# A three-layer decoder in one kernel: four steps of its batch pipeline stand elsewhere in the engines' orders

## The reference

```
x = layernorm(x + conv5(x) + b + decayed_sum(x) @ W.T)              # retention and a convolution of 5 taps
# mLSTM cell, q = x, k = v = context, 8 heads of 64
ig, fg = [q, k, v] @ gate weights;  cs = cumsum(log_sigmoid(fg))
D = exp(cs[s] - cs[t] + ig[t] - max);  S = (q k^T / 8) * D          # t <= s
h = S / (max(|sum S|, exp(-max)) + eps) @ v
x = layernorm(x + layernorm(h) * ln_scale)
# 32 experts, 2 per token, capacity 160
stats = [mean, std, min, max, norm, share of near zeros] of x
probs = softmax(gelu([x, stats] @ r1.T + r1_b) @ r2.T)              # router
x = layernorm(x + experts(x, top 2 of probs) + small experts per pair)
```

## Time and profile before

| | us |
|---|---|
| median of three runs (1981.58, 1985.99, 1986.74) | 1985.99 |
| profiled execution, its own time | 1981.9 |
| its span | 1979.7 |
| TensorE matmul busy | 1671.1 (84%) |
| VectorE busy | 788.4 (40%) |
| ScalarE busy | 481.3 (24%) |
| GpSimd busy | 308.0 (16%) |

### The profile page before, as it was taken

How to read it: one execution, slowest core, us unless ns; L and a number is a source line. 1 busy time by engine, 2 the same in 40 slices (tenths; PEclk the granted TensorE clock), 3 DMA queues, 4 the chain that set the end, 5 groups by cost and what they waited for, 6 DMA issues and landing times.

```text
span 1979.7 us, 28321 instructions
## 1 busy us (share of the span) xinstructions
PE 1671.1 (84%) x10930; PEld 1406.3 (71%) x10930; DVE 788.4 (40%) x1731; ACT 481.3 (24%) x1165; POOL 308.0 (16%) x368
## 2 busy tenths in 40 slices
PE   3689889888898742249999999999999999999980
PEld 1355546545455522238999999999999999999980
DVE  4669777787774555681111111011111111110117
ACT  1546363553644220001111111111111111111100
POOL 1111111111111110001111212121211112121212
PEclk9789997898988565579999999999999999999995
DMA  5203213022120116004666666767666676767519
GB/s 138 61 4 107 64 43 107 36 72 65 43 86 1 43 43 287 0 0 157 240 237 254 221 256 213 276 214 277 216 254 243 232 257 219 257 217 275 189 14 339
DMA packets 88669, 309.70 MB, mean 156 GB/s; under 512 B 42326, under 2 KB 42332, under 8 KB 79260
## 3 DMA queue, kind: packets, MB, share of 16 engines
q1 hardware_dynamic: 78876, 287.87, 38.7%
q0 software_dynamic: 9728, 20.98, 6.0%
HBM read 272.52 MB, written 36.31 MB: 156 GB/s over the span
## 4 chain that ended last, share of the span: by engine, by line
PE 54%; DVE 7%; issue 1%; DMA 1%; ACT 1%; POOL 0%; POOLq 0%; DVEq 0%; ACTq 0%
PE bank L814 32%; PE bank L827 16%; DVE arena L1425 2%; PE banks L793 1%; PE banks L794 1%; DVE arena L1554 1%; PE bank L766 1%; PE banks L836 1%; PE banks L838 1%; DVE arena L1564 1%; PE bank L677 0%; DVE arena L1495 0%; PE bank L781 0%; DMA arena<-acc_rows 0%; DVE arena L1432 0%
## 5 line engine op out<-in xcount | busy, mean ns | idle before, releaser
L814 PE MATMUL bank<-arena 128*128 128x160 f32 x4608 | 638.1, 300 | 0.6 <-issue 0.6
L814 PEld LDWEIGHTS bank<-arena 128*128 128x128 f32 x4608 | 630.3, 190 | 1.1 <-issue 0.7
L1537 DVE TENSOR_TENSOR arena<-arena,bank 128x160 f32<-128x160 f32 x256 | 82.1, 321 | 828.3 <-ACT arena L1080 826.4
L827 PE MATMUL bank<-arena 128*128 128x160 f32 x2304 | 321.5, 300 | 0.9 <-DVE arena L1539 0.9
L827 PEld LDWEIGHTS bank<-arena 128*128 128x128 f32 x2304 | 313.8, 190 | 2.4 <-issue 1.2
L1710 POOL DMA_INDIRECT acc_rows<-arena,keep x64 | 95.5, 1493 | 831.3 <-DVE arena L1526 795.0
L1080 ACT ACTIVATE arena<-bank 128x160 f32<-128x160 f32 x288 | 87.4, 303 | 562.6 <-PE bank L814 562.6
L550 PE MATMUL bank<-arena 128*128 128x512 f32 x256 | 125.3, 635 | 31.3 <-DVE arena L1127 31.3
L550 PEld LDWEIGHTS bank<-arena 128*128 128x128 f32 x256 | 51.5, 206 | 87.0 <-issue 83.8
L1127 DVE SCALAR_TENSOR_TENSOR arena<-arena 128x512 f32<-128x512 f32 x128 | 110.2, 861 | 3.4
L1086 ACT ACTIVATE arena<-bank 128x320 f32<-128x320 f32 x64 | 28.0, 437 | 292.4 <-PE bank L827 292.4
(11 more groups left out here) (216 smaller groups left out, 1850.3 us busy)
## 6 DMA issues: line engine op xcount, KB each, us to landing
arena<-in_wup SPq DMA_DIRECT2D x32, 4096.0 KB, 12.5
arena<-in_wdn SPq DMA_DIRECT2D x32, 2048.0 KB, 8.5
arena<-in_aup SPq DMA_DIRECT2D x32, 512.0 KB, 11.6
arena<-in_xT SPq DMA_DIRECT2D x8, 1024.0 KB, 5.3
arena<-in_kT SPq DMA_DIRECT2D x8, 1024.0 KB, 7.3
arena<-in_v SPq DMA_DIRECT2D x32, 256.0 KB, 7.7
x_rows<-arena SPq DMA_DIRECT2D x8, 1024.0 KB, 4.4
acc_rows<-arena SPq DMA_DIRECT2D x8, 1024.0 KB, 6.7
```

What stands on the lines that cost most here:

```text
L814: m = pe.matmul(u[:, g * CAP:(g + 1) * CAP], w, xeT[:, c, :], start=(c == 0), stop=(c == C - 1))
L827: m = pe.matmul(Db[k][:, c * CAP:(c + 1) * CAP], w, hact[:, j, :], start=(j == 0), stop=(j == J))
L1537: dve.tensor_tensor(hact[:, j, :], sg[k], u, ALU.mult).then_inc(up_v(f"mul{j}"), 1)
```

## The change

Five places in the order of calls change, and one operation goes to another engine.

- VectorE: `scale_queries(n - 1, 0)` stands between the two halves of the second norm, after `norm2_stats` and ahead of `norm3_sum`. It stood after `norm3_sum` and two `norm1_stats`.
- TensorE: `gates_k` stood ahead of decay row 1. Its first two chunks are now between row tiles 1 and 2 of `queries`, its last two behind tile 3. `gates_q` stood behind max row 7. Its first two chunks are now between tiles 1 and 2 of `router_in`, its last two behind max row 7.
- TensorE: `router_stats` stands ahead of the hidden layer's products, not behind them. ScalarE's copy of that row stands after `gates_1` and no longer after `gates_4`.
- ScalarE: `squares` stands ahead of `raw_rows(n, 3)` and head 5's exponentials, not behind them. `router_1` stands ahead of `inputs(n + 1, 2)`.
- `weigh_values` is on VectorE, behind `scale_queries(n - 1, 3)` and ahead of `retained(n + 1, 3)`. It was the last call of GpSimd's step. Who waited for GpSimd's step now waits for VectorE's.

```diff
@@ tensor: queries, gates_k, gates_q, router_in take the tiles or chunks that they run
-            def queries(b):
-                for tb in range(TB):
+            def queries(b, tiles):
+                for tb in tiles:
...
-            def gates_k(b):
-                pe.wait_ge(ld_k[b.slot], b.landed())
-                pe.wait_ge(*st_v.at("S2", b - 1))
-                for c in range(C):
+            def gates_k(b, chunks):
+                if chunks[0] == 0:
+                    pe.wait_ge(ld_k[b.slot], b.landed())
+                    pe.wait_ge(*st_v.at("S2", b - 1))
+                for c in chunks:
...
@@ tensor: state
-                pe.wait_ge(*st_p.at("vw", b))
+                pe.wait_ge(*st_v.at("vw", b))
...
@@ tensor: step
                     broadcast_max(n - 1, 5)
-                if a:
-                    gates_k(n)
                 if s:
                     broadcast_decay(n - 1, 1)
                     values(n - 1, 1)
                     scores(n - 1, 2)
                 if a:
-                    queries(n)
+                    queries(n, (0, 1))
+                    gates_k(n, (0, 1))
+                    queries(n, (2, 3))
+                    gates_k(n, (2, 3))
                 if s:
                     broadcast_max(n - 1, 6)
                 if r:
-                    router_in(n - 2, a)
+                    router_in(n - 2, a, (0, 1))
+                if a:
+                    gates_q(n, (0, 1))
+                if r:
+                    router_in(n - 2, a, (2, 3))
                 if s:
                     broadcast_max(n - 1, 7)
                 if a:
-                    gates_q(n)
+                    gates_q(n, (2, 3))
...
                 if r:
+                    router_stats(n - 2, a)
                     router_hidden(n - 2, 0)
                     router_hidden(n - 2, 1)
-                    router_stats(n - 2, a)
                     router_hidden_stats(n - 2)
@@ scalar: step
                     decays(n - 1, 4)
+                if r:
+                    squares(n - 2)
                 if a:
                     raw_rows(n, 3)
                 if s:
                     decays(n - 1, 5)
-                if r:
-                    squares(n - 2)
...
                     decays(n - 1, 6)
+                if r:
+                    router_1(n - 2, a)
                 if x1:
                     inputs(n + 1, 2)
-                if r:
-                    router_1(n - 2, a)
...
                     gates_1(n)
+                if r:
+                    router_stats(n - 2)
+                if a:
                     gates_3(n)
                     gates_4(n)
                 if r:
-                    router_stats(n - 2)
@@ vector: step
                     norm2_stats(n - 2)
+                if s:
+                    scale_queries(n - 1, 0)
+                if r:
                     norm3_sum(n - 2)
                 if a:
                     norm1_stats(n, 0)
                     norm1_stats(n, 1)
-                if s:
-                    scale_queries(n - 1, 0)
...
                     scale_queries(n - 1, 3)
+                if a:
+                    weigh_values(n)
                 if x1:
                     retained(n + 1, 3)
@@ pool: step
-                if a:
-                    weigh_values(n)
```

More of the change, by code:

```diff
@@ L311, in decoder_kernel @@
         qs_v = steps("qscale_vector", [f"qs{j}" for j in range(NP)])
-        st_p = steps("state_pool", ["vw"])
         st_t = steps("state_tensor", ["r"] + [f"p{q}" for q in range(TB - 1)])
         st_a = steps("state_scalar", ["S0"])
-        st_v = steps("state_vector", ["m1", "S1", "m2", "S2"])
+        st_v = steps("state_vector", ["vw", "m1", "S1", "m2", "S2"])
         ev_v = steps("ev_vector", [x for j in range(NP) for x in (f"neg{j}", f"den{j}", f"eps{j}", f"rec{j}", f"out{j}")])
@@ L563, in queries, with gates_q @@
                     m.then_inc(qt_t(f"t{tb}"), 1)
-            def gates_k(b):
-                pe.wait_ge(ld_k[b.slot], b.landed())
-                pe.wait_ge(*st_v.at("S2", b - 1))
-                for c in range(C):
+            def gates_k(b, chunks):
[3 more added lines that the diff above has]
+                for c in chunks:
                     m = pe.matmul(Tb[0:GATE, :], wgk[:, c, :], kT[b.slot][:, c, :], start=(c == 0), stop=False)
-                m.then_inc(ga_t("gates_k"), 1)
-            def gates_q(b):
+                if chunks[-1] == C - 1:
+                    m.then_inc(ga_t("gates_k"), 1)
+            def gates_q(b, chunks):
                 pe.wait_ge(*qt_a.at(f"q{TB - 1}", b))
-                for c in range(C):
+                for c in chunks:
                     m = pe.matmul(Tb[0:GATE, :], wgq[:, c, :], qT[b.slot][:, c, :], start=False, stop=(c == C - 1))
-                m.then_inc(ga_t("gates"), 1)
+                if chunks[-1] == C - 1:
+                    m.then_inc(ga_t("gates"), 1)
             def gate_columns(b):
@@ L644, in values, with router_in @@
                 m.then_inc(pv_t(f"pv{j}"), 1)
-            def router_in(b, before):
-                for tb in range(TB):
+            def router_in(b, before, tiles):
+                for tb in tiles:
                     w = Wb[tb % 2]
@@ L943, in gates_5 @@
                 act.wait_ge(*at_a.at(f"exp{NH - 1}", b - 2))
-                act.wait_ge(*st_p.at("vw", b - 1))
+                act.wait_ge(*st_v.at("vw", b - 1))
                 cols = Tb[:, 0:TB * GROW].rearrange("p (a g) -> p a g", a=TB)
@@ L1157, in scale_queries, with weigh_values @@
                 dve.tensor_tensor(qs[j % 2], qT[b.slot][:, j, P:T], Bb[:, 0:INT], ALU.mult).then_inc(qs_v(f"qs{j}"), 1)
+            def weigh_values(b):
+                dve.wait_ge(*ga_a.at("w", b))
+                dve.wait_ge(*st_t.at(f"p{TB - 2}", b - 1))
+                dve.wait_ge(ld_v[b.slot], b.landed(TB))
+                src = va[b.slot][:, 0:TB - 1, 0:NH * VW].rearrange("p a (h w) -> p a h w", h=NH)
+                dve.tensor_tensor(vw, src, wcol[:, 0:TB - 1].unsqueeze(3).to_broadcast([P, TB - 1, NH, VW]), ALU.mult)\
+                    .then_inc(st_v("vw"), 1)
             def later_states(b):
```

7 lines of the change are left out of this document (removed).

## The result

| | before | after |
|---|---|---|
| median of 8 runs each, us | 1982.7 (1980.6 to 1993.4) | 1998.0 (1992.7 to 1999.4) |
| ratio, 95% interval | | 1.0065 (1.0046 to 1.0084) |
| profiled execution: time / span, us | 1981.9 / 1979.7 | 1992.7 / 1990.6 |
| mean granted clock of TensorE | 0.90 | 0.893 |

A forecast was written before the change was run, and what follows sets the result against it. No engine full: one chain through VectorE, ScalarE and TensorE bounds it. Steps 3 to 6 -1, step 2 +7.1, 7 +2.7, 8 +0.7, 9 +5.0, 0 and 1 +0.4: +15 on 1981.9, 1997; forecast 1999 us, range 1963 to 2009.

The forecast's parts named there:

- Up to decay row 1: TensorE's decay row 1 waits for head 5's exponentials behind the squares: W + 30.7, 3.0 us earlier than before.
- W: Start of the weighting of heads 0 and 1 on VectorE; a pipeline step runs from W to the next W.
- The clock behind the pause: TensorE from decay row 1: 8.7 us to the scores' end, clock low for 11 us, decay row 2 after 23.05 us.
- G: Start of the weighting of heads 6 and 7 within a step; forecast 4.75 us after decay row 2.
- G and the end of the step: Logits at G + 11.6; next W at G + 23.65, with 1.0 us added for the clock, against 25.45 before.
- Step 2: Early scaling waits for decay row 0: decay row 1 +1.1 us, decay row 1 to 2 23.05 us; +7.1 us overall.
- Steps 8 and 9: Pipeline end: step 8 +0.7 us (squares +1.2, statistics -0.5); step 9 +5.0 us, hidden layer waiting for GpSimd's standard deviation.
- Value weights: Product on VectorE some 1.75 us, not 3.00 on GpSimd; VectorE reaches next W at G + 22.3, worth nothing by itself.
- Rival one: Faster: clock holds or returns at once after decay row 1; 76.3 us a step, 1957 to 1961 us; chance 0.2.
- Rival two: No difference: low clock ends with the scores, half of 4.5 us lost; 79.2 us a step, 1977 to 1981; chance 0.2.
- Rival three: Worse: low clock also takes value products after decay row 2 and hidden layer's start, 3 us each; 2012 us; chance 0.1.

The follow-up runs named there:

- squares_back: The changed kernel with the squares again behind head 5's exponentials: 1985.3 us, ratio 1.0019 to the kernel before.
- keys_ahead: The changed kernel with all four key products of the gates again ahead of decay row 1: 1966.4 us, ratio 0.9904 to the kernel before.
- keys_twice: The changed kernel with the four key products also done, unused, in their old place ahead of decay row 1: 1973.5 us, ratio 0.9929 to the kernel before.
- values_pool: keys_ahead with the weighting of the values back on GpSimd: 1963.1 us, ratio 0.9890 to the kernel before.
- best2p: values_pool with third queries scaled ahead of retention tile 2, step 9's statistics late, and unused extra scores ahead of the logits: 1922.7 us, ratio 0.9703.
- edges: The changed kernel with the first scaled queries late in step 2 and the statistics late in step 9: 1998.5 us, ratio 1.0072 to the kernel before.
- best2: keys_ahead with both moves of edges, third queries scaled ahead of retention tile 2, and unused extra scores ahead of the logits: 1944.8 us, ratio 0.9805.
- both_filled: keys_twice with the scores of heads 0 and 1 also computed twice, unused, ahead of the logits: 1960.1 us, ratio 0.9893 to the kernel before.
- b_keys: The kernel before with only the key products moved, to between the halves of the row transposes: 1999.2 us, ratio 1.0058.

## Why the prediction was right

**The total.** Forecast 1999 us, measured 1998.0. The hit is closer than the sum was, and in part luck: I added 15 us to a profiled execution, and the profiled execution of the changed kernel came out 10.8 us longer. The parts are off by up to 2.7 us each, both ways.

**Up to decay row 1.** Forecast W + 30.7, measured 428.43 - 397.77 = 30.66. The wait of 3.27 us went, and the exponentials of head 4 did not come sooner. The squares in front of head 5 set the rest; with them behind, squares_back has W + 28.2 in steps 3 and 6, and 30.3 in steps 4 and 5, which began at the low clock. The changed kernel's step 6 began so too and has W + 33.3.

**The clock behind the pause.** Forecast 8.5 to 8.7 us for decay row 1 to the end of the scores, measured 8.52 at a clock of 0.50 (1.2 GHz); keys_ahead and keys_twice have 4.6 at 1.00 (2.4 GHz). I had the clock low for 11 us. The trace has it back at the key products, 438.53 - 428.43 = 10.1 us on, so decay row 1 to 2 took 22.24 us and not 23.05.

**G and the end of the step.** Decay row 2 to G 4.95 (forecast 4.75). Logits at G + 11.65 (11.6), next W at G + 24.0 (23.65). The 1.0 us that I added for the clock was too little: behind the pause of 1.41 us the value products take 3.71 instead of 2.0 us, the state products 1.55 instead of 0.9 and the scores 2.08 instead of 1.1. The kernel before had most of this already (2.87, 1.55 and 2.08 us, from 466.17 in its step 5). Values_pool and best2p, with the clock held, have W at G + 19.9 in step 5. Step 5 came out at 81.86 us against 82.1, or 82.6 with the half microsecond that I added.

**Step 2.** The total is right (+7.8 for +7.1) and its split is not. Decay row 1 came 2.9 us later than before, not 1.1. I had let the squares in front of head 5 cost nothing there, and they land on the path: squares_back has decay row 1 at W + 29.15 and the changed kernel at W + 31.4. The rest, decay row 1 to 2, took 22.0 us and not 23.05. VectorE's wait for decay row 0 was 3.15 us (forecast 2.95).

**Steps 8 and 9.** The mis-sized term is step 8: -2.0 for +0.7. Decay row 1 came 1.2 us later, as I said. But before, the products behind decay row 2 and the start of the hidden layer ran at the low clock. TensorE from decay row 2 to G, and in the hidden layer, of before and then after:

```profile
677.90:685.90 8.00, 7.97 (x47) 7.03 (x48) 0.55 (x1) 0.00 (x0) 0.00 (x0) 0.55 0.00 0
685.90:697.50 11.60, 10.92 (x25) 4.44 (x25) 2.53 (x6) 1.30 (x2) 0.00 (x0) 0.87 0.00 1
```

```profile
687.50:692.30 4.80, 4.74 (x48) 3.96 (x49) 0.56 (x2) 0.00 (x1) 0.00 (x0) 1.00 0.00 0
692.30:701.20 8.90, 8.90 (x24) 3.80 (x22) 2.53 (x6) 1.25 (x2) 0.00 (x0) 1.00 0.00 0
```

After the change the low stretch fell elsewhere: decay row 3 came at W + 56.2 instead of 61.1, although decay row 1 was later, so 6 us came back. The last value products then met the low clock, and 2.9 us of it were gone again by the transposes of step 9. I had left this step's clock as it was. In step 9 the hidden layer waits 6.13 us for the statistics, as forecast; it cost 4.3 us for 5.0, and edges gets 3.3 of it back.

**Value weights.** "Worth nothing by itself" held at the low clock: values_pool against keys_ahead. The number under it, VectorE at the next W at G + 22.3, was right too (22.03 in best2, 22.56 in both_filled), and it decides as soon as the clock holds; then the move costs 2.2 us a step.

**The rivals.** Rival one asked what the change would do at a held clock, and answered 1957 to 1961 us (its four steps of 76.3 us are 26 us less than before, not 25); both_filled took 1960.1. Its mechanism was right and its condition wrong: pauses of 1.2 to 3.4 us can take the clock down. What I put down in its favour was read too short. After the 3.27 us in step 5 of the kernel before, the next products do take 0.89 us, but the row tile 1.9 us on does not run at the full clock; it takes 5.20 us, and 3.70 us in step 5 of the changed kernel:

```profile
412.85 5.20 PE L550 MATMUL bank<-arena 128*128 128x512 f32 x8
```

So the waits of the kernel before had a price in clock too, and the change gave that back here. The Trainium skill, "TensorE: Matmul & The Clock Gate", section "What's actually happening", gives under 1% for the ramp at the start of a kernel; the low stretches here come back in every step, and by the ratios of both_filled and the changed kernel they cost 1.7%, so that advice does not carry over to them. Rival two had the low clock end with the scores and half of its price hidden. It ended soon after them (the transposes took 1.65 us for 1.09), but hardly anything was hidden: decay row 1 to 2 took 22.2 us, and 18.1 in both_filled. Rival three's mechanism, a low clock in the hidden layer too, shows in two steps of edges (decay row 3 at W + 70.6 instead of 66.8), not in the changed kernel.

What stays open: what sets where in a step the clock falls when several pauses of 1 to 3 us follow one another. b_keys and edges show that it moves with small shifts elsewhere; no run here predicts it. The squares, the first scaled queries, the query products and the router's copy were not tried alone on the kernel before, so no run shares out the loss among all the parts.

## What to carry to other kernels

Before taking a wait away or moving work out of a queue, list TensorE's idle stretches after the move, the short ones too, and price the work behind each at both clock levels; work that stood in what would be a pause was paying for itself. Where independent work can't be moved into a pause, matmuls whose result nobody reads may be cheaper than the pause. Work that waits for a late operand belongs on the engine whose queue holds nothing urgent behind it, even if that engine is slower.

## What the runs showed of the hardware

Filling the pauses of the changed kernel with some 40 more matmuls a step made it 1.7% faster (0.9893 / 1.0065), and best2p, whose steady steps run at a clock of 1.00 in another order, took 3.0% less than the kernel before. Two pauses of 1.38 and 1.23 us close together were followed by 9.85 us at 1.2 GHz, from 425.55 to 435.40 (squares_back), while one of 1.64 us with 3.6 us of products behind it was not (keys_ahead). One of 1.29 us was followed by the low clock in step 7 of b_keys and not in its step 5. The same program had steps of 74.4 and 78.95 us in one execution by nothing but the clock. The product of 1560 columns took 1.78 us on VectorE, 2.80 us on GpSimd beside a VectorE that was mostly idle and 3.00 us beside the taps, which then took 5.50 us instead of 3.09. One tap of the four took the whole difference: 3.17 us and not 0.75, up to 0.55 us after GpSimd's product ended.
